# Moving the key-value state matmuls and the numerators behind the first gate/up product of a fused linear-attention and FFN kernel

## The reference, cut to what matters

```
xn    = layernorm(x)
q,k,v = xn @ Wq.T, xn @ Wk.T, xn @ Wv.T           # 16 heads of 16
q, k  = elu(q) + 1, elu(k) + 1
state, ksum = einsum('bhnd,bhne->bhde', k, v), k.sum(tokens)
attn  = (q @ state) / max(q . ksum, 1e-6)
local = 3-tap depthwise convolution of xn over the tokens
branch 1 = (attn + local) @ Wp.T + bp
branch 2 = (silu(xn @ Wg.T) * (xn @ Wu.T)) @ Wd.T  # 256 -> 768 -> 256
out   = x + branch 1 + branch 2
```

## Time and profile before

| what | value |
|---|---|
| median of three runs | 484.11 us |
| the profiled execution | 483.59 us |
| its span, first to last instruction | 482.0 us |
| TensorE clock granted | 1.000 |
| PE busy | 470.9 us, 98% of the span |
| DVE busy | 419.6 us, 87% |
| ACT busy | 348.0 us, 72% |
| POOL busy | 169.9 us, 35% |

### The profile page before, as it was taken

The page is one execution under the profiler, slowest core; times in us unless marked ns, Lnnn a source line. Parts: engine busy times, 40 slices in busy tenths (PEclk is TensorE's granted clock), DMA queues, the critical chain, the costliest instruction groups (busy, mean ns, idle before and its releaser), DMA issues.

```text
span 482.0 us, 11019 instructions
## 1 busy us (share of the span) xinstructions
PE 470.9 (98%) x3957; PEld 263.6 (55%) x3957; DVE 419.6 (87%) x762; ACT 348.0 (72%) x538; POOL 169.9 (35%) x168
## 2 busy tenths in 40 slices
PE   7989999999999999999999999999999999999997
PEld 6545454745546464564745546474564646556455
DVE  6898788988979899797989979799897989978997
ACT  2869777777685787768678686877768588676952
POOL 6465416260432615135160521625034260512043
DMA  8655345344634535364344525534463353436033
GB/s 297 217 84 137 45 107 113 90 132 74 184 52 105 143 66 171 54 162 89 87 133 84 174 44 125 136 87 131 65 172 67 96 141 67 132 45 131 1 88 133
DMA packets 78429, 53.76 MB, mean 112 GB/s; under 512 B 35008, under 2 KB 77888, under 8 KB 78400
## 3 DMA queue, kind: packets, MB, share of 16 engines
q1 hardware_dynamic: 68992, 44.06, 34.0%
q0 software_dynamic: 8448, 8.39, 11.7%
q10 hardware_dynamic: 960, 0.92, 0.6%
HBM read 20.32 MB, written 8.39 MB: 60 GB/s over the span
## 4 chain that ended last, share of the span: by engine, by line
PE 88%; DVE 5%; issue 2%; ACT 2%; DMA 2%; SPq 0%; DVEq 0%
PE ps L1169 17%; PE ps L1349 16%; PE ps L1275 16%; PE ps L1330 16%; PE ps L1339 15%; PE ps L1239 3%; PE ps L1292 2%; DVE hl L1032 2%; DMA wu_int<-in_L_ffn_w_up_dram 2%; PE ps L1227 2%; DVE hid L1026 1%; PE ps L1212 1%; ACT act_g L642 1%; DVE rden L910 0%; ACT hh L650 0%
## 5 line engine op out<-in xcount | busy, mean ns | idle before, releaser
L1026 DVE SCALAR_TENSOR_TENSOR hid<-act_g,scales,ps 128x512 f32<-128x512 f32 x96 | 71.5, 745 | 36.9 <-ACT act_g L642 35.7
L642 ACT ACTIVATE act_g<-ps,scales 128x512 f32<-128x512 f32 x96 | 65.9, 686 | 39.7 <-PE ps L1339 39.2
L1032 DVE TENSOR_TENSOR hl<-hid,hh 128x512 f16<-128x512 f32 x96 | 69.9, 728 | 1.5
L650 ACT ACTIVATE hh<-hid 128x512 f16<-128x512 f32 x96 | 59.7, 622 | 11.1 <-DVE hid L1026 11.1
L412 POOL TENSOR_TENSOR xT<-xh,xl 128x1024 f32<-128x1024 f16 x15 | 31.8, 2121 | 92.9 <-issue 92.9
L377 POOL TENSOR_SCALAR xn<-x_in,neg_mean,rstd 128x256 f32<-128x256 f32 x62 | 61.3, 998 | 4.3 <-POOL rstd L384 4.2
L1330 PE MATMUL ps<-xh,g_wh 128*128 128x512 f16 x192 | 57.6, 382 | 1.1 <-DVE hid L1026 1.0
L1330 PE MATMUL ps<-xh,u_wh 128*128 128x512 f16 x192 | 57.1, 379 | 0.0
L1339 PE MATMUL ps<-xl,u_wh 128*128 128x512 f16 x192 | 57.1, 379 | 0.0
L1339 PE MATMUL ps<-xl,g_wh 128*128 128x512 f16 x192 | 57.1, 379 | 0.0
L1349 PE MATMUL ps<-d_wh,hh 128*128 128x256 f16 x384 | 53.0, 273 | 1.2 <-ACT hh L650 0.9
(11 more groups left out here) (173 smaller groups left out, 939.3 us busy)
## 6 DMA issues: line engine op xcount, KB each, us to landing
xb<-bp_sb SPq DMA_DIRECT2D x16, 512.0 KB, 3.6
xb<-in_L_attn_x_dram POOLq DMA_DIRECT2D x16, 512.0 KB, 5.9
over_den<-rden SPq DMA_DIRECT2D x64, 128.0 KB, 2.7
x_in<-in_L_attn_x_dram SPq DMA_DIRECT2D x15, 512.0 KB, 4.5
out_dram<-out_sb SPq DMA_DIRECT2D x14, 512.0 KB, 2.9
wg_int<-in_L_ffn_w_gate_dram SPq DMA_DIRECT2D x1, 768.0 KB, 6.1
wu_int<-in_L_ffn_w_up_dram SPq DMA_DIRECT2D x1, 768.0 KB, 7.6
wd_int<-in_L_ffn_w_down_dram SPq DMA_DIRECT2D x1, 768.0 KB, 10.3
```

The source lines that it names most:

```text
L642: nc.scalar.activation(act_g[:, j % 2, :], ps[:, gate_bank(j), :], ACT.Silu, scale=silu_in).then_inc(silu_ready, 1)
L650: nc.scalar.activation(hh[:, j, :], hid[:, j % 2, :], ACT.Copy).then_inc(hh_ready, 1)
L1026: nc.vector.scalar_tensor_tensor(out=hid[:, j % 2, :], in0=act_g[:, j % 2, :], scalar=h_mul, in1=ps[:, gate_bank(j) + 1, :], op0=ALU.mult, ...
L1032: nc.vector.tensor_tensor(hl[:, j, :], hid[:, j % 2, :], hh[:, j, :], ALU.subtract).then_inc(hl_ready, 1)
```

## The change

On PE, in every step but (0, 0), `gate_up(0)` comes before `accumulate(0)`; `accumulate(0)`, `accumulate(1)` and, where there is attention, `numerators` follow each other, and then comes `gate_up(1)`. On DVE, in attended steps that work ahead, both `put_y` stand behind `hidden(0)`, no longer in front of it. In the last step, (7, 1), DVE keeps its order. Nothing is computed differently.

```diff
@@ DVE, step @@
                 if attend:
                     put_k(1)
-                    put_y(b - 1, c, 0, NUM)
-                    put_y(b - 1, c, 1, NUM)
+                    if not ahead:
+                        put_y(b - 1, c, 0, NUM)
+                        put_y(b - 1, c, 1, NUM)
                 if ahead:
                     for j in range(J):
                         hidden(j)
+                        if attend and j == 0:
+                            put_y(b - 1, c, 0, NUM)
+                            put_y(b - 1, c, 1, NUM)
                         if j >= 1:
                             hidden_low(j - 1)
@@ PE, step @@
                 project_kv(1)
                 project_q()
+                gate_up(0)
                 accumulate(0)
+                accumulate(1)
                 if attend:
                     numerators(b - 1, c, NUM)
-                gate_up(0)
-                accumulate(1)
                 gate_up(1)
```

## The result

The changed kernel takes 485.61 us (median of 8 runs, 485.05 to 486.25), the kernel before 484.08 us beside it (median of 8, 483.53 to 484.54). The ratio is 1.0031, with a 95% interval of 1.0023 to 1.0040: slower by 0.3%, 1.53 us. The forecast was 485.4.

What follows compares the result with a forecast made beforehand. PE, busy for 98% of the span, was taken to bound the kernel. Terms -0.42 + 0.10 + 0.14 + 1.49 = +1.31 us on the profiled 483.59, plus 0.52 to the median, gave 485.4 us; range 483.6 to 486.5.

Steps and rivals of the forecast that it cites:

- The order on PE: PE in step (4, 1): `gate_up(0)` ahead of the state groups saves one seam behind and one in front, 0.22 us.
- The new wait for the keys: PE's second state group in step (4, 1): it waits for `put_k(1)` and starts 0.13 us late.
- The moved sums: DVE behind `hidden(0)`: the sums' 1.31 us use up 1.28 us of idle time, leaving 0.06 us gained at `gate_up(3)`.
- The other steps: Steps besides the last: seven gain 0.42 us together, five loop steps with c = 0 lose 0.1, (1, 0) loses 0.14.
- The seven gains: Steps with c = 1 from (1, 1) to (6, 1), and (7, 0): 0.06 us gained in each, -0.42 us together.
- the forecast's bullet on loop steps with c = 0: Five loop steps, reckoned from (5, 0): `hidden(0)` 0.08 us later, `gate_up(3)` 0.02 us later than before, +0.1 us together.
- The last step: Step (7, 1): later numerators delay DVE's queue and PE waits for the state before the denominators, +1.49 us, the largest term.
- the drains decide: Rival: 13 attended steps up to (7, 0) keep 0.22 us each, less 1.49 in the last: 482.7 us; chance 0.1.
- Only the keys hold PE: Rival: sums fit, the second state group's wait stays; twelve steps gain 0.09 us each, 484.7 us; chance 0.2.
- The last step absorbs it: Rival: steady steps as forecast, but DVE's chain in (7, 1) has room; -0.2 us, 483.9 us; chance 0.1.
- DVE's lateness grows: Rival: every step is 0.08 us late, or waits behind a sum cost as much; 1.0 us more, 486.4 us; chance 0.15.
- The forecast's count of changes by that rule: Tiling-mode changes on PE per attended step, each draining TensorE: five before the change and three after.

Runs made afterwards that it cites:

- k: j, but on PE in attended steps up to (7, 0) `gate_up(0)` stands between `accumulate(0)` and `accumulate(1)`, one more pair of seams; 485.70 us.
- e: Changed kernel with two DVE edits: one sum before and one behind `hidden(0)` in steps that work ahead, `put_k(1)` before the two taps; 483.81 us.
- f: e, but PE keeps the order of the kernel before in the last step; 482.18 us, ratio 0.9955.
- d: Changed kernel, but DVE runs `put_k(1)` before the two taps; 485.09 us.
- a: Changed kernel, but PE keeps the order of the kernel before in the last step, (7, 1); 484.08 us, ratio 1.0005.
- b: Changed kernel, but in the last step DVE runs the second sum behind `hidden(0)`; 485.81 us.
- c: Changed kernel, but in steps that work ahead DVE runs the first sum before `hidden(0)` and the second behind it; 485.27 us.
- g: Kernel before with only the PE part of the change, DVE keeping both sums before `hidden(0)`; 492.92 us, ratio 1.0177.
- j: f, but the first sum stands behind `hidden(0)` and the second behind `hidden_low(1)` at j = 2; 483.68 us.
- l: Kernel before with the hardware loop's turn shifted by one step, (2, 0) and (6, 1) written out; 486.27 us in one run.

## Why the prediction was right

The time (485.4 against 485.61, difference 1.31 against 1.53 by the medians and 1.49 in the two stretches) and the mechanism held, by the forecast's own steps:

- **The order on PE.** The forecast put `gate_up(1)` at 6.22 us behind `project_q` with the late keys; it is at 6.23. The seam by itself was put at 0.22 us and is worth 0.17 to 0.18 (k, and (1, 1) with 6.13 against 6.31). The term was mis-sized because the second group was given the 0.27 us from first to last start, and takes 0.31. This cost the forecast nothing in the loop, since DVE held PE anyway, and 0.05 us at `put_y` in the last step; it made the expectations of e and f too high by some 0.5 us.
- **The new wait for the keys.** Seen: 0.1 us in (4, 1), 0.41 us in (1, 0), where the second group starts alone at 78.15 (the timeline of PE in the changed kernel, below). d removes it and gains only 0.49 us, nearly all in (1, 0) and (3, 0), as the sums still hold.

```profile
77.28 0.46 PE L1296 MATMUL ps<-v_sb,k_sb 128*32 128x33 f32 x32
78.15 0.46 PE L1296 MATMUL ps<-v_sb,k_sb 128*32 128x33 f32 x32 [0.41 <-DVE k_sb L983]
```

- **The moved sums.** `hidden(0)`, both sums and `hidden(1)` without idle time, 0.06 us left with c = 1. e against d shows that they were what held: with the split the steps fall to 28.50 us.
- **The other steps.** Forecast -0.42 + 0.10 + 0.14 = -0.18 us, measured +0.03. The seven gains were 0.05 to 0.06, (1, 0) lost 0.16 where 0.14 was forecast. Of the five loop steps with c = 0 four lost 0.03 to 0.04 and not 0.02, and (3, 0) lost 0.11: there the keys end at 4.96 us behind `project_q`, 0.2 later than in (4, 1), which the forecast's bullet on loop steps with c = 0 overlooked by taking (5, 0) for all five.
- **The last step.** Forecast +1.49, measured 38.10 - 36.64 = 1.46 us, and a gives it back whole. That it fits to 0.03 us is in part luck: `put_y` moved by 2.04 us and not 1.99, `put_q` by 1.74 and not 1.69, but there was more room in front of `hidden(0)` than the 0.20 us counted, and it moved by 1.45. b shows that DVE's chain carries it and PE's idle time at the denominators doesn't.

Of the rivals, "the drains decide" needs both DVE edits before it shows. Its own figure, 482.7 us, had the last step's loss in it, so e is its counterpart, at 483.81; without that loss it would be 481.2, and f is at 482.18. Either way it promised about 1 us more than came, for the smaller seam and the late wake. "Only the keys hold PE" was worked out as 1.08 less 0.14 us gained up to (7, 0). d refutes it: with the keys early, `gate_up(1)` comes 0.1 us sooner and `gate_up(3)` stays at 9.72 or 9.73 us. In a step with c = 1 as it stands the rival was off by only 0.03 us (0.06 gained and not 0.09). c, where the keys stay late and the sums are split, gains 0.33 us on the kernel before, since the late wake comes in. "The last step absorbs it" is refuted by a. "DVE's lateness grows" did not come in the changed kernel and did in c, e, f and g, as soon as a sum stood waiting ahead of `hidden(0)`.

The drain of which the Trainium skill speaks (TensorEngine Tiling (Array Packing), Tiling Modes, Key Properties) agrees with k: a pair of changes between whole-array and tiled matmuls costs 0.17 us here. It decides the time only where nobody else holds PE. The forecast's count of changes by that rule, five before and three after, left out the two around `denominators` in each attended step; they stand in both kernels, so the difference of two holds.

## What to carry to other kernels

On an engine that is 98% busy a saving between instructions is real, but it reaches the end only if every other engine that PE meets within the step has that much slack too; find each such cover in the timeline (here `put_k(1)`, some 0.1 us short, and the sums, 0.13 us short once the keys are early: `gate_up(3)` at 9.72 us in d and 9.59 in e) and move them together, because each alone hides the other. When an order is changed in all steps and its partner edit in all but one, cost that one step by itself: here it held the whole loss. In an in-order queue look at how long an instruction that waits holds up one behind it that the critical engine needs: both sums ahead of `hidden(0)` cost 7.65 us up to (7, 0) in g, one sum there cost 0.16 us in five steps of f, and moving it away in j cost more than that elsewhere.

## What the runs showed of the hardware

- Changing from whole-array matmuls to 32-column tiles and back costs 0.17 us for the pair of changes (j against k, thirteen steps, 2.24 us).
- A DVE instruction that waits with its engine idle woke 0.24 us later in the first step of a loop turn than in the second (f: 1.43 against 1.19 us behind the start of the numerators), and `hidden(0)` 0.09 us later (before: 7.03 against 6.94 us behind `project_q`); the steps outside the loop show neither. With the loop shifted (l), the steps in the loop were late in both places of a turn. The cause is open.
- `hl`, a DVE subtraction of 0.68 us, takes 0.91 to 1.43 us when it starts while POOL's addition into `local` is under way, and ends 0.55 us after that addition in all 28 cases of the fourteen traces. An addition that starts during `hl` takes 1.44 to 1.74 us and not 1.26 to 1.29. `hidden` and the reciprocal stay at 0.75 and 1.75 us beside them.
